# One additional maximum over the partitions at the start of GpSimd's queue

## The reference

```python
x = x + tanh(g_xattn[0]) * cross_attention(layernorm(x), ctx)      # one head of 256, 77 keys
x = x + tanh(g_ffn[0]) * quantised_gated_ffn(layernorm(x))         # 256 -> 768 -> 256
x = x + tanh(g_xattn[1]) * cross_attention_16_heads(layernorm(x), ctx, bias)
x = x + tanh(g_ffn[1]) * mixture_of_8_experts(layernorm(x))        # 256 -> 512 -> 256
```

```python
def act_qdq(x):
    qmax = 2.0 ** 15 - 1.0
    scale = jnp.maximum(jnp.max(jnp.abs(x)) / qmax, 1e-12)
    return jnp.clip(jnp.round(x / scale), -qmax - 1.0, qmax) * scale
x = act_qdq(x); up = act_qdq(x @ w_up.T); gate = act_qdq(x @ w_gate.T)
gate = act_qdq(gate * fixed_qdq_u16(sigmoid(gate))); o = act_qdq(gate * up)
```

## Time and profile before

| | |
|---|---|
| median of 3 runs | 591.76 us (589.72 to 592.52) |
| the profiled execution | 593.56 us, span 591.8 us |
| TensorE busy | 470.6 us (80% of the span) |
| VectorE, ScalarE, GpSimd busy | 334.1, 254.8, 130.0 us |
| chain that ended last | TensorE 69%, VectorE 11%, "issue" 11%, ScalarE 4%, GpSimd 1% |
| granted TensorE clock, mean | 0.872 |
| GpSimd: maxima over the partitions | 5, together 1.8 us busy |

### The profile page before, as it was taken

How to read it: one execution, slowest core, us unless ns; L and a number is a source line. 1 busy time by engine, 2 the same in 40 slices (tenths; PEclk the granted TensorE clock), 3 DMA queues, 4 the chain that set the end, 5 groups by cost and what they waited for, 6 DMA issues and landing times.

```text
span 591.8 us, 8071 instructions
## 1 busy us (share of the span) xinstructions
PE 470.6 (80%) x2478; PEld 306.6 (52%) x2479; DVE 334.1 (56%) x714; ACT 254.8 (43%) x459; POOL 130.0 (22%) x151
## 2 busy tenths in 40 slices
PE   3777739998995000989899999999997359999993
PEld 2566624445442000878556566666665225776672
DVE  1376558252899699434445545555547724555552
ACT  1324234546786484500445554555544223333220
POOL 4134016603000000011565000010001053444221
PEclk9955558998999555999899999999999659999998
DMA  8700000000000001000019800000003321222000
GB/s 254 195 2 1 0 2 1 3 0 0 0 0 1 0 0 43 0 2 1 1 40 387 325 1 1 2 1 1 1 0 105 112 63 53 59 67 60 24 24 0
DMA packets 27287, 27.06 MB, mean 46 GB/s; under 512 B 11631, under 2 KB 23452, under 8 KB 27005
## 3 DMA queue, kind: packets, MB, share of 16 engines
q1 hardware_dynamic: 25053, 21.59, 11.5%
q0 software_dynamic: 2208, 5.14, 3.0%
HBM read 22.48 MB, written 5.15 MB: 47 GB/s over the span
## 4 chain that ended last, share of the span: by engine, by line
PE 69%; DVE 11%; issue 11%; ACT 4%; POOL 1%; DMA 1%; DVEq 1%; SPq 1%; POOLq 0%; ACTq 0%
PE bank L1399 55%; PE bank L1618 6%; PE bank L1446 3%; PE bank L1764 2%; DVE big_g L1130 1%; PE bank L1636 1%; ACT big_u L740 1%; PE bank L1491 1%; DVE amU L1142 1%; PE bank L1515 1%; DVE amZ L1136 1%; DVE big_u L981 1%; ACT yT L740 1%; DMA gates<-in_g_ffn 1%; DVE stat L974 1%
## 5 line engine op out<-in xcount | busy, mean ns | idle before, releaser
L1399 PE MATMUL bank<-yT,ffn_w 128*128 x192 | 86.4, 613 | 3.3 <-ACTq L796 2.7
L1399 PE MATMUL bank<-ffn_w,big_u 128*128 128x256 f32 x192 | 44.0, 391 | 49.1 <-ACT big_u L740 49.0
L740 ACT ACTIVATE big_u<-bank 77x512 f32<-77x512 f32 (+4 forms) x103 | 58.1, 578 | 22.9 <-PE bank L1474 9.6
L1399 PEld LDWEIGHTS bank<-ffn_w,big_u 128*128 128x128 f32 x192 | 37.6, 197 | 55.4 <-ACT big_u L740 49.9
L1399 PEld LDWEIGHTS bank<-yT,ffn_w 128*128 128x128 f32 x192 | 37.5, 197 | 51.0 <-issue 49.8
L1243 DVE TENSOR_REDUCE mx<-bank 128x4 f32<-128x308 f32 x64 | 30.6, 479 | 55.6 <-PE bank L1399 55.6
L896 ACT ACTIVATE big_g<-big_g 128x308 f32<-128x308 f32 x64 | 29.4, 459 | 56.3 <-DVE big_g L1244 56.3
L1399 PE MATMUL bank<-k_blockdiag,big_g 128*128 128x308 f32 x128 | 45.8, 440 | 0.7 <-ACT yT L740 0.7
L1399 PE MATMUL bank<-big_g,yT 128*128 x92 | 44.1, 623 | 0.7 <-issue 0.7
L1399 PE MATMUL bank<-big_u,yT 128*128 x184 | 41.8, 380 | 1.6 <-DVE yT L1362 1.6
L1618 PE MATMUL bank<-ident,big_g 128*77 128x128 f32 x256 | 41.0, 284 | 0.3
(11 more groups left out here) (249 smaller groups left out, 836.3 us busy)
## 6 DMA issues: line engine op xcount, KB each, us to landing
big_g<-in_L_ffn_W SPq DMA_DIRECT2D x1, 4096.0 KB, 16.9
big_u<-in_L_ffn_W SPq DMA_DIRECT2D x1, 4096.0 KB, 26.3
x_rows<-in_x SPq DMA_DIRECT2D x2, 1024.0 KB, 8.2
ffn_w<-in_L_ffn_b SPq DMA_DIRECT2D x1, 2048.0 KB, 24.9
tmp<-bias_by_distance SPq DMA_DIRECT2D x2, 616.0 KB, 4.9
token_rows<-x_rows SPq DMA_DIRECT2D x1, 1032.0 KB, 7.9
tmp<-in_L_ffn_b SPq DMA_DIRECT2D x1, 1024.0 KB, 5.3
token_rows<-x_rows SPq DMA_DIRECT2D x1, 774.0 KB, 9.6
```

The costliest lines, as they stand in the source:

```text
L740: act.activation(out_, in_, ACT.Copy, **k).then_inc(done, 1)
L1399: return pe.matmul(out_, lhsT=lhsT, rhs=rhs, start=first, stop=last)
```

## The change

A new tile `warm_r` of 128 x 2 words. Behind the last constant, GpSimd writes zeros into its first column, waits for that write (`c.link`), and takes the maximum over the 128 partitions of that column into the second. Nothing reads the result. All that follows in GpSimd's queue, `rstds_a(0)` first, now stands behind it.

```diff
         warm = sb("warm", [1, 1])
+        warm_r = sb("warm_r", [P, 2])
...
             pool.tensor_copy(vals[:, :, 1], self_i)
             pool.tensor_copy(rank[:, :], rank_i).then_inc(s.pool_consts, 1)
+            c.link(pool.memset(warm_r[:, 0:1], 0.0))
+            pool.partition_all_reduce(warm_r[:, 1:2], warm_r[:, 0:1], P, bass.bass_isa.ReduceOp.max)
             def rstds(t, mv_ready, done, per):
```

## The result

The changed kernel takes 597.63 us as the median of 8 runs (596.12 to 606.97), against 591.24 us for the kernel before, measured beside it. The ratio is 1.0115, with a 95% interval of 1.0083 to 1.0147: it is 5 to 9 us slower. The ratio is taken without the slow executions, of which the changed kernel had one, 606.97 us. Measured once more later, the ratio was 1.0084 (1.0052 to 1.0116). The time lies within the stated range of 589.7 to 599.0, but 5.6 us above the likeliest value of 592.0. What came was the slower rival, priced at 598.5 us and given a chance of 0.27.

A forecast was written before the change was run, and what follows sets the result against it. TensorE holds 69% of the chain that ended last; GpSimd matters only where another engine waits for it. Two loads nearly used up a 5.84 us cover: 591.76 + 0.2, rounded to 592.0 us, range 589.7 to 599.

The forecast's parts named there:

- the slower rival: Input DMAs slow the two new code loads at the kernel's start; at factor 1.5, 6.5 us more, 598.5; chance 0.27.
- The sum itself: Two quiet loads eat the first 1/sqrt's cover of 5.84 us almost exactly; +0.2 us taken, giving 592.0 us.
- "no change": Outcome within about 0.5%, or 3 us, of the kernel before; chance 0.70.
- its own sign of being wrong on the slow side: VectorE's first L1003, which uses the first 1/sqrt, starting at 26 us or later; 22.8 to 23.1 was expected.
- That the added maximum brings a change of code and back: At GpSimd's start, MODIFY_POOL_CONFIG pairs near 8.05 and 14.05 us load the maximum's code, then the other code for `rstds_a(0)`.
- That nothing is saved at the first real maximum: MX at L633 needs its load again, 5.65 us behind its MODIFY; even a free load gives at most 0.1 us.
- cold and then warm: Faster rival: MX's 3.08 us is a first-call price that the new maximum removes; 589.0 if ScalarE's copies were no bound.
- the cover of 5.84 us: First 1/sqrt ready at 16.94 us, but VectorE's L1003, released by TensorE, wants it only at 22.78.
- The price of the two loads: At GpSimd's start, 5.65 us towards the maximum and 7.0 to 7.6 us back, together 12.65 to 13.25 us.
- the table load of ScalarE: Evidence against slowed loads: 1.283 us at 8.5 us within the input DMA rush, the same as at 142.9 us.
- The rival and its point of decision: Loads slowed by input DMAs decide from factor 1.23, where 3 us are added; slowed by more, chance 0.27.
- The wait between MODIFY and operation: MODIFY for the load back either ahead of the wait for `mv_a`, +0 to 0.25 us, or behind it, +1.2 to 1.8.

## Why the prediction was right or wrong

The time came within the range because the range was stretched far into a rival with a chance of 0.27. The sum itself, +0.2 us, failed, and so did "no change" with its 0.70. The prediction had named its own sign of being wrong on the slow side, a first L1003 at 26 us or later, and it came at 27.64. So its mechanism held and one size in it didn't.

**That the added maximum brings a change of code and back: right.** Both MODIFY pairs came where they were put (8.0 and 17.1 us, predicted 8.05 and 14.05 plus the slower load). The row of maxima with something and with nothing between them confirms the reading in both directions. One sentence of it went too far: MODIFY pairs don't stand at four lines alone, and not every pair is followed by a load. In the kernel before, `affine_select` (L551) starts 0.1 us behind its pair at 1.4 us, and so do the three later rounds of L591 behind theirs, at 265.1, 275.1 and 286.3 us, when the code had been brought back in the first round. The pair marks a possible change. The idle time behind it shows whether there was one.

**That nothing is saved at the first real maximum: right.** It waits 5.8 us again, because `tensor_scalar` and `tensor_tensor` in between have brought the other code back. In the kernel with two pairs the second way to the maximum cost 5.6 us, so "cold and then warm" falls as a rival. That ScalarE would have bound the gain to 0.1 us wasn't tried.

**Who waits, and the cover of 5.84 us: right.** VectorE's L1003 lost its cover, its releaser changed from TensorE to GpSimd, and the run with ordinary work in place of the loads lost the same 5 us. The delay ran through the groups one for one, 4.9 to 5.2 us, up to the clock's gain in the third. On top came 0.35 us at MX (the gate's first matmul at 92.54 in place of 88.91, 3.63 us, against 3.29 us at L1075, ahead of it): the maximum's arm was later than ScalarE's this time, by 0.29 us of idle ahead of the rounding of `yT`. The two arms are as close as the earlier trace rows had them.

**The price of the two loads: wrong, and this is the step that failed.** I summed them at 12.65 to 13.25 us, the price of quiet places, and got a delay of 0 to 0.25 us. They took 8.78 + 9.06 = 17.84 us. That is a factor of 1.35 to 1.41, 1.55 on the way there and 1.2 to 1.3 on the way back. With a factor of 1.4 in the sum of the prediction, 13.0 x 0.4 = 5.2 us are added, and the delay is 5.4 us. The second and third groups show 5.2. The decision was made by the table load of ScalarE, which took the same time in and out of the rush. I called it the nearest row in kind. It isn't: that load of tables took 1.283 us with and without traffic, and the run with traffic made at 79 us shows that the load of GpSimd's code grows from 5.65 to 11.4 us. The Trainium skill (GPSIMD Engine Reference, section Terminology) says that these libraries are brought in by DMA; the lengthened gaps agree, though no queue of the profile shows the transfers: from 8 to 26 us the changed kernel has packets of the input DMAs' queue alone. The Trainium skill's 6 us for a load (GPSIMD Engine Reference, section Instruction dispatch) agrees with 5.5 to 6.1 us towards the maximum in quiet. It is short for the way back, 6.8 to 7.8, and for either in the traffic of the changed kernel, 8.8 and 9.1, so there the measurement decides.

**The rival and its point of decision: right.** Factor 1.23 adds 3 us, and 1.37 adds 5. The rival's 598.5 at factor 1.5 stands against 597.63, closer than it deserves: the delay in the profiles is 5 to 5.5 us and the second ratio gives 5.0, so some of the 6.4 us between the two medians is spread. The chance of 0.27 was too low. A cover that the sum used up to the last tenth should not have carried 0.64.

**The wait between MODIFY and operation.** The prediction left both placements open. The moved maximum shows what it can be worth: with a wait of its own ahead of the operation, the load back began only when the operand was there, and VectorE's normalisation came 5.2 us later.

## What to carry to other kernels

Before adding a GpSimd operation, look in its queue for instructions that no line has written, and read the idle time behind them. In this kernel an operation of 0.4 us that needs other code cost two loads, 13 us in quiet and 18 us in traffic, and doing it once early doesn't make the later one cheaper if anything in between needs the first code again. If it must be there, put it where GpSimd has that much time before its next customer, directly followed by one cheap operation that asks for the old code, so that the way back doesn't start behind a wait. And when a sum says that a cover is used up to the last tenth, forecast the side towards which the unknown term can only grow.

## What the runs showed of the hardware that I had not expected

- The load of GpSimd's code is slowed by DMA traffic of others: 5.5 to 6.1 us and 6.8 to 7.8 us in quiet; 8.3 to 8.8 and 9.1 to 9.9 us in the first 27 us at a DMA share of 1.06 to 1.30; 11.4 and 13.2 us beside copies of 4 MB. The share doesn't predict the length: two loads that began at 18.5 us took 5.9 and 6.3 us at 1.15 and 1.37.
- A stall taken away from the path in the quantised network didn't make the kernel faster. Its chain was ahead by some 3 us, and in one of two profiles the granted clock stayed at 1.2 GHz for 24 us behind it, instead of 7. Between two groups of the changed kernel's profiled execution the clock alone gave back 2.3 us of the delay (5.17 to 2.87), so a change of a few us is to be read from where events start, and its time from many executions.
